# The second expert's values taken from the sum of both experts' activations

## The reference

```
t  = rms_norm(x);  weights = top 2 of softmax(t @ gate), normed
h1[e] = t @ w1 + 2 (t @ a1[e]) @ b1[e];   h3[e] likewise with w3, a3, b3
act[e] = silu(h1[e]) * h3[e]
out = sum over e of weights[e] * (act[e] @ w2 + 2 (act[e] @ a2[e]) @ b2[e])
```

## Time and profile before

| | us |
|---|---|
| median of 3 runs | 1060.06 |
| lowest, highest | 1056.37, 1061.72 |
| profiled execution | 1054.69 |
| its span, first to last instruction | 1053.0 |

### The profile page before, as it was taken

How to read it: one execution, slowest core, us unless ns; L and a number is a source line. 1 busy time by engine, 2 the same in 40 slices (tenths; PEclk the granted TensorE clock), 3 DMA queues, 4 the chain that set the end, 5 groups by cost and what they waited for, 6 DMA issues and landing times. The chain is left out here.

```text
span 1053.0 us, 15574 instructions
## 1 busy us (share of the span) xinstructions
PE 980.6 (93%) x4429; PEld 669.9 (64%) x4429; DVE 711.2 (68%) x2140; ACT 507.9 (48%) x1039; POOL 500.1 (47%) x485
## 2 busy tenths in 40 slices
PE   3999999999999999999999999899988999889993
PEld 2766667656565665656566656477864667648873
DVE  5787779788786877879797776445543667634542
ACT  3433454655646556564453332144534777515451
POOL 3456555554535545354654655524451155423443
PEclk9999999999999999999999999999999999989997
DMA  6069000000000000000000002146534000015651
GB/s 181 1 284 415 3 1 1 1 1 1 1 0 2 0 1 1 1 0 1 12 3 9 11 11 71 39 137 197 166 94 140 1 22 22 22 42 178 194 174 34
DMA packets 42900, 65.12 MB, mean 62 GB/s; under 512 B 7153, under 2 KB 25121, under 8 KB 40640
## 3 DMA queue, kind: packets, MB, share of 16 engines
q1 hardware_dynamic: 37824, 55.59, 16.1%
q0 software_dynamic: 4992, 8.54, 2.4%
HBM read 37.20 MB, written 28.74 MB: 63 GB/s over the span
## 5 line engine op out<-in xcount | busy, mean ns | idle before, releaser
L362 PE MATMUL bank<-split 128*128 128x512 f32 x416 | 206.9, 497 | 7.8 <-DVE ud L1267 4.1
L364 PE MATMUL bank<-split 128*128 128x512 f32 x416 | 165.2, 397 | 0.0
L363 PE MATMUL bank<-split 128*128 128x512 f32 x416 | 164.8, 396 | 0.0
L863 ACT ACTIVATE sil<-bank 128x512 f32<-128x512 f32 x128 | 76.2, 595 | 116.0 <-PE bank L364 115.2
L1644 POOL TENSOR_TENSOR gsum<-act 128x512 f32<-128x512 f32 x64 | 84.9, 1327 | 81.5 <-DVE act L1203 81.4
L421 PE MATMUL bank<-act,a 128*128 128x512 f32 x256 | 117.6, 592 | 0.0
L362 PEld LDWEIGHTS bank<-split 128*128 128x128 f32 x416 | 79.5, 191 | 48.8 <-issue 17.4
L1199 DVE TENSOR_TENSOR act<-bank,sil 128x512 f32<-128x512 f32 x128 | 87.8, 686 | 17.2 <-PE bank L364 14.2
L363 PEld LDWEIGHTS bank<-split 128*128 128x128 f32 x416 | 79.9, 192 | 28.3 <-issue 18.6
L688 PE MATMUL bank<-xlT,e 128*128 128x256 f32 x368 | 91.2, 392 | 5.1 <-ACT xlT L1068 2.7
L1203 DVE TENSOR_TENSOR act<-act,wT 128x512 f32<-128x512 f32 x128 | 91.7, 716 | 4.4
(11 more groups left out here) (283 smaller groups left out, 1957.6 us busy)
## 6 DMA issues: line engine op xcount, KB each, us to landing
e<-e_dram SPq DMA_DIRECT2D x92, 256.0 KB, 3.1
rows_in<-yw SPq DMA_DIRECT2D x17, 1056.0 KB, 17.8
xin<-rows_in SPq DMA_DIRECT2D x46, 132.0 KB, 3.0
x<-rows_out SPq DMA_DIRECT2D x8, 256.0 KB, 4.7
rows_in<-yw,slot_i POOLq DMA_INDIRECT x64, 2.3
rows_out<-ob,ids POOLq DMA_INDIRECT x46, 2.3
out<-ob,ids POOLq DMA_INDIRECT x46, 2.4
act<-b_dram SPq DMA_DIRECT2D x2, 256.0 KB, 3.1
```

Source lines behind the costliest of these rows:

```text
L362: mm(dst, w[0], m[0], start=start, stop=False, **more)
L363: mm(dst, w[0], m[1], start=False, stop=False, **more)
L364: return mm(dst, w[1], m[0], start=False, stop=stop, **more)
L863: af(sil[(k - 1) % 2][:, :], bank[BH1[STEPS[k - 1][0] % 2]][:, :], ACT.Silu).then_inc(silu_done.sem, 1)
```

## The change

The second expert's values are no longer computed from its own activations. `value_sum` multiplies a2 by the sum of both, and the second expert's part comes out as (values of the sum) - (values of the first), so that DVE masks the first expert's values by the difference of the two masks (`mdT`) and POOL subtracts. The sum is made in place of the second expert's activations, then split once: ACT copies the high part (`sums_high`, four a slot), POOL subtracts the low part (`sums_low`, four a slot), and both `value_sum` and `down` use mm3 on it. w2 and a2 are split too, in slot 0 (two copies on ACT, two subtractions on POOL). `down(3)` moves to the next slot, behind `a_den`; on POOL `up_low(0)` moves ahead of `total(3)`. mdT has two buffers and the first mask has one. Seven weights of the second layer are loaded after the last h product, into space that the split weights have left.

```diff
-        mT = [[sb(f"mT{i}{k}", [P, S]) for k in range(2)] for i in range(2)]
-        mdT = sb("mdT", [P, S])
+        mT0 = sb("mT0", [P, S]); mT1 = [sb(f"mT1{i}", [P, S]) for i in range(2)]; mdT = [sb(f"mdT{i}", [P, S]) for i in range(2)]
...
+            gs = [(part(33 + j), part(j)) for j in range(J)]
+            w2s, a2s = parts(37), parts(39)
...
+        act1 = [sb(f"act1{j}", [P, S]) for j in range(J)]
...
+        late_loads = whole(("wk_l1", wk_l1), ("wq_l1", wq_l1), ("wv_l1", wv_l1), ("waT", waT), ("wbT", wbT))
+        late_loads += [(eb1r[:, :], d["eb1"].rearrange("o (n p) -> (o n) p", p=P)), (eb2r[:, :], d["eb2"].rearrange("o (n p) -> (o n) p", p=P))]
...
+                  (w2s, w2[:, :], 1.0), (a2s, a2[:, :, :].rearrange("p j d -> p (j d)"), 1.0)]
+        LOW_DVE, LOW_POOL, LOW_LATE = (0, 1, 3, 5), (2, 4), (6, 7)
@@ sync
                     sp.wait_ge(*h3_ready(MAINS - 1))
+                    for dst, src in late_loads:
+                        sp.dma_start(dst, src).then_inc(late_loaded.sem, 16)
@@ tensor
-                        last = mm(bank[BV][:, :], a2[:, j, :], act_[e][j][:, :], start=j == 0, stop=j == J - 1)
+                        last = mm(bank[BV][:, :], a2[:, j, :], act0[j][:, :], start=j == 0, stop=j == J - 1)
...
+                def value_sum():
+                    if l is None:
+                        return
+                    pe.wait_ge(*r_done(l, 1))
+                    pe.wait_ge(*sum_low(l))
+                    if l == 0:
+                        pe.wait_ge(weight_rest.sem, len(LOW_POOL) + 2)
+                    for j in range(J):
+                        last = mm3(bank[BV][:, :], tuple(w[:, rows(j)] for w in a2s), gs[j], j == 0, j == J - 1)
+                    last.then_inc(v_ready.sem, 1)
+
+                def down(n, j):
+                    if n is None:
+                        return
                     if j == 0:
-                        pe.wait_ge(*xf_done(g - 1))
-                    pe.wait_ge(*summed(g, j + 1))
-                    mm(bank[BOUT][:, :], w2[:, j, :], gsum[j % 2][:, :], start=j == 0, stop=False).then_inc(w2_used.sem, 1)
+                        pe.wait_ge(*xf_done(n - 1))
+                        if n == 0:
+                            pe.wait_ge(weight_rest.sem, len(LOW_POOL) + 1)
+                    pe.wait_ge(*sum_low(n, j + 1))
+                    mm3(bank[BOUT][:, :], tuple(w[:, rows(j)] for w in w2s), gs[j], j == 0, False)
...
                 a_den()
+                down(l, 3)
                 h(3, 2)
                 pre_T()
                 a_back()
-                value(1, range(J))
+                value_sum()
...
                 a_gate(1)
-                down(2)
+                down(g, 2)
                 a_gate(2)
-                down(3)
                 a_gate(3)
@@ scalar
                     if n == 0:
+                        act.wait_ge(*u_masked(q - 1))
+                    if n == 1:
                         act.wait_ge(*r_done(q - 2))
...
+                def sums_high(j):
+                    if g is None:
+                        return
+                    act.wait_ge(*summed(g, j + 1))
+                    act.wait_ge(*v_ready(g - 1))
+                    af(gs[j][0], act1[j][:, :], ACT.Copy).then_inc(sum_high.sem, 1)
...
                 silu(2)
+                sum_weights()
...
                 silu(5)
+                sums_high(0)
...
                 silu(6)
+                sums_high(1)
...
                 silu(8)
+                sums_high(2)
                 up_high(0)
                 a_square(1)
                 a_square(2)
                 a_gates()
                 up_high(1)
+                sums_high(3)
                 a_norm(1)
@@ vector
-                    v.tensor_tensor(r1[:, :], bank[BV][:, :], mT[g % 2][0][:, :], ALU.mult).then_inc(r_done.sem, 1)
+                    v.tensor_tensor(r1[:, :], bank[BV][:, :], mdT[g % 2][:, :], ALU.mult).then_inc(r_done.sem, 1)
@@ gpsimd
                     pool.wait_ge(*weighted(g, STEP[j, 1]))
-                    pool.wait_ge(*w2_used(g, j - 1))
-                    pool.tensor_tensor(out=gsum[j % 2][:, :], in0=act_[0][j][:, :], in1=act_[1][j][:, :], op=ALU.add).then_inc(summed.sem, 1)
+                    pool.tensor_tensor(out=act1[j][:, :], in0=act0[j][:, :], in1=act1[j][:, :], op=ALU.add).then_inc(summed.sem, 1)
+
+                def sums_low(j):
+                    if g is None:
+                        return
+                    pool.wait_ge(*sum_high(g, j + 1))
+                    pool.tensor_tensor(out=gs[j][1], in0=act1[j][:, :], in1=gs[j][0].bitcast(F32), op=ALU.subtract).then_inc(sum_low.sem, 1)
...
-                    pool.tensor_tensor(out=r1[:, :], in0=r1[:, :], in1=r2[:, :], op=ALU.add).then_inc(r_ready.sem, 1)
+                    pool.tensor_tensor(out=r1[:, :], in0=r2[:, :], in1=r1[:, :], op=ALU.subtract).then_inc(r_ready.sem, 1)
...
                 total(1)
+                sum_weights_low()
+                sums_low(0)
                 f_scale()
+                sums_low(1)
                 mask_diff()
                 a_scale()
                 r_scale(s.r_stat)
                 total(2)
+                sums_low(2)
+                up_low(0)
                 total(3)
-                up_low(0)
                 up_low(1)
+                sums_low(3)
                 a_product()
```

More of the change, by code:

```diff
@@ L148, in build @@
         xnT = sb("xnT", [P, S])
+        lower = xnT[:, 0:P]
         lg = sb("lg", [P, T, E]); gt = sb("gt", [P, T, E]); pr = sb("pr", [P, T, E]); mx1 = sb("mx1", [P, 2, T])
@@ L155, in build, with part, parts @@
         rf = sb("rf", [P, T])
+        rows_in = nc.dram_tensor("rows_in", [NROWS, W], F32, kind="Internal").ap()
+        rows_out = nc.dram_tensor("rows_out", [NCH * S, P], F32, kind="Internal").ap()
+        stats_l = sb("stats_l", [P, T, 6]); part_l = sb("part_l", [P, 4, T])
+        mv_l = [sb(f"mv_l{i}", [P, T]) for i in range(2)]; sc_l = [sb(f"sc_l{i}", [P, 2, T]) for i in range(2)]
+        yn_l = [yn_f, yn_a]
+        yT, zT, pr_, pT = [tT, hT], mT1, act0[0:2], act0[2:4]
+        vu = [z, h2]
+        nb_l = sb("nb_l", [P, T]); nmx = sb("nmx", [P, 2]); rs = sb("rs", [P, 2]); rsi = sb("rsi", [P, T])
+        with nc.sbuf_tensor("split", [P, 41 * S], F32R) as split:
+            def part(n):
+                return split[:, n * S:(n + 1) * S]
+            def parts(n):
+                return part(n), part(n + 1)
+            gs = [(part(33 + j), part(j)) for j in range(J)]
+            w1s, w3s, b1s, b3s = (parts(4 + 2 * i) for i in range(4))
+            w2s, a2s = parts(37), parts(39)
+            a1s, a3s = (tuple(split[:, 12 * S + (k + i) * P:12 * S + (k + i + 1) * P] for k in range(2)) for i in (0, 2))
+            ts = [parts(13), parts(15)]
+            uas = [[parts(17 + 8 * p + 2 * i) for i in range(2)] for p in range(2)]
+            uds = [[parts(21 + 8 * p + 2 * i) for i in range(2)] for p in range(2)]
+        act1 = [sb(f"act1{j}", [P, S]) for j in range(J)]
+        act_ = [act0, act1]
+        a1, a3 = act1[0][:, 0:P], act1[0][:, P:2 * P]
+        wk_l1 = sb("wk_l1", [P, P]); wq_l1 = sb("wq_l1", [P, P]); wv_l1 = sb("wv_l1", [P, P])
+        waT = sb("waT", [P, P]); wbT = sb("wbT", [P, P])
+        wak = sb("wak", [P, P]); gmat = sb("gmat", [P, P]); wuT = sb("wuT", [P, P])
         cnt = sb("cnt", [P, E]); cnt_i = sb("cnt_i", [P, E], I32); nt_i = sb("nt_i", [P, E], I32); ntf = sb("ntf", [P, E])
@@ L652, in first_layer @@
                 mask(0)
-                down(0)
+                down(g, 0)
                 a_mid(1)
@@ L658, in first_layer @@
                 a_mid(2)
-                down(1)
+                down(g, 1)
                 mask(2)
@@ L666, in first_layer @@
                 h(3, 8)
-                value(0, (0, 1))
+                value((0, 1))
                 a_gate(0)
@@ L906, in mask, with sum_weights @@
                     ins.then_inc(maskT_saved.sem, 1)
+                def sum_weights():
+                    if g != 0:
+                        return
+                    for n in LOW_LATE:
+                        dst, w, f = SPLITS[n]
+                        af(dst[0], w, ACT.Copy, scale=f).then_inc(weight_high.sem, 1)
+                def sums_high(j):
[4 more added lines that the diff above has]
+                    af(gs[j][0], act1[j][:, :], ACT.Copy).then_inc(sum_high.sem, 1)
                 def up_high(i):
```

83 lines of the change are left out of this document (31 added, 52 removed).

## The result

The changed kernel takes 1103.42 us (median of 4 runs, 1100.97 to 1105.75), the kernel before 1059.44 beside it (4 runs, 1056.37 to 1061.72): a ratio of 1.0417 [1.0381, 1.0453]. The forecast was 1071.8, with a range that ended at 1086. The direction was right; the size was not: +11.7 us forecast, +44.0 measured. The profiled executions took 1054.69 (span 1053.0) and 1105.75 (span 1104.0), so they lie 51 us apart where the medians lie 44: that of before is 5 under its median, that of the changed kernel 2 over.

What follows compares the result with a forecast made beforehand. PE, DVE and ACT were taken as within a microsecond of each other, DVE ending last after the change. Terms 6.0 + 0 + 3.9 + 0 + 1.8 = +11.7 us gave 1066.4 profiled, 1071.8 median; range 1047 to 1086.

Steps and rivals of the forecast that it cites:

- +1.0 in slots 5 to 10, 6.0 us: Gated slots 5 to 10: one new POOL op holding DVE, with ACT's 0.6 mostly beside it, costs +1.0 each, 6.0 us.
- taken as 0: Slots 3 and 4: DVE has spare time; PE's -0.34 against ACT's +0.6, counted as 0.
- POOL's subtractions and DVE: Four more 1.28 us POOL ops per slot, each holding DVE 0 to 1.28; bound +0 to +2.5 per gated slot.
- Rival (c): Port takes it all: both new ops held in each of six slots, +23.7 us, 1083.8; chance 0.13.
- ACT's copies: Four per slot at 0.63; the third, queued before up_high(0), waits for total(2): +0.6 in a gated slot if DVE is on time.
- down(3) moved: Gated slots: moved behind a_den, it leaves a gap nothing fills and costs 0.69 where PE has no gap.
- Slots 0 to 2: First stage without gates: PE waits for POOL's low parts, +0.5 in slot 0, +1.7 each in 1 and 2, +3.9 total.
- Slots 11 to 14: PE's lead about 4.7, -1.4 to +0.3 each; `ud` later by 0 to 1.3: 0 for the four, bounds -5 and +5.
- The way out: End of the layer, after slot 15: POOL's row scatter 2.2 late, some regained from slot 15's products, +1.8.
- At nothing: Late weights, two-buffer mask difference and new addresses count nothing; a few us once without cover, addresses up to 1 us either way.
- Rival (a): PE sets every slot, holds fall into idle time: -11.6 us, 1048.5; chance 0.22.
- (b): Effects cancel: gated slots lose 2.4, way out 1.8, eight other slots win 4 together: 0, 1060; chance 0.2.

Runs made afterwards that it cites:

- experiment 3: Changed kernel without POOL's four subtractions a slot, PE taking the high part in place of the low: 1064.35 us, 1.0042 of the kernel before.
- experiment 2: Kernel before with the new algebra alone (plain products, no splits, copies or subtractions) and down(3) moved into the next slot: 1068.65 us, 1.0087 of before.
- experiment 1: Kernel before with the new algebra alone: plain products, no splits, copies or subtractions, down(3) in its old place: 1059.90 us, 1.0003 of before.
- experiment 9: Changed kernel without subtractions, down(3) back, copies 3 and 4 between sigmoids, POOL's old order, high part again as third pass: 1049.34 us, 0.9900 of before.
- experiment 4: Changed kernel with copies and subtractions elsewhere in the queues and down(2) also in the next slot: 1100.23 us, 1.0386 of the kernel before.
- experiment 5: Changed kernel with POOL's subtractions in place, but PE neither waits for nor reads them: 1101.72 us, 1.0394 of the kernel before.
- experiment 6: Changed kernel with each subtraction replaced by a POOL power on 128x5, low part left out: 1076.57 us, 1.0161 of the kernel before.
- experiment 7: Changed kernel with keep-busy products on PE ahead of the second and fourth gate product: 1103.95 us, 1.0405 of the kernel before.
- experiment 10: Changed kernel's arithmetic with subtractions on DVE, all four down products in the next slot, later copies between sigmoids, POOL's old order: 1099.55 us, 1.0383 of before.
- experiment 11: Changed kernel with subtractions for j = 0 and 1 kept, those for j = 2 and 3 left out: 1089.60 us, 1.0257 of the kernel before.
- experiment 8: Changed kernel with two passes, no subtractions, down(3) back, copies 3 and 4 between sigmoids, POOL's old order: 1038.72 us, 0.9804 of the kernel before.
- experiment 12: Changed kernel with subtractions for j = 2 and 3 kept, those for j = 0 and 1 left out: 1080.63 us, 1.0189 of the kernel before.

## Why the prediction was wrong, step by step

The failed step is the term **"+1.0 in slots 5 to 10, 6.0 us"**, and behind it the sentence "nearest is one op held" for a slot that had four new ones. At full clock slots 5 to 10 lost 14.3 in place of 6.0, 2.4 a slot. Slots 3 and 4, "taken as 0", lost 6.7: there the spare time on DVE that the prediction named did not cover. Of these 21 us, 6.4 come without the subtractions (experiment 3) and about 14.6 with them.

- **POOL's subtractions and DVE.** The mechanism was named, and its size was taken from one held operation in the earlier trace rows. Measured by leaving them out: 39.1 us, 2.4 per slot over 16 slots, in all stages: 22.0 in slots 3 to 10, 7.3 in slots 0 to 2, 7.8 in slots 11 to 14 (sums of the same stretches in the changed kernel and experiment 3). Rival (c), "both new ops held", was nearest in kind and number, with 1083.8; but it too had only the gated slots 5 to 10 lose by it, and looked only at sums_low(0) and (1). The leaky step beside sums_low(2) (684 ns on average before, 1044 after) was not looked for. What I should have added up is the chance of a hold for every wide POOL operation, since DVE works through most of the slot.
- **The rule on the shared ports.** The Trainium skill says ("SBUF — State Buffer", section "SBUF: two separate sides") that of a VectorE instruction with two SBUF inputs and a GpSimd instruction that reads SBUF the later one stands still for the other's whole instruction. The traces agree where POOL reads wide tiles (1.25 for a 128x4 operation that began 0.06 after a mask difference of 1.29), and `ua` with one input from PSUM is not held (683 ns). They differ for tiny tiles: the weighting at 343.64, with both inputs in SBUF, took its usual 0.69 beside the power that ran from 342.49 to 344.50, and 64 powers of 1.40 us added nothing to DVE's busy time (715.6 and 714.4). Here the measurement decides: a long POOL instruction on a tiny tile did not hold DVE for as long as its row says.
- **ACT's copies.** "The third is the dear one, +0.6": the replay had ACT wait 0.97 for total(2) (318.38 to 319.35). It waits 1.52 in slot 7 of experiment 3 and 2.09 in the changed kernel, because total(2) itself came late by DVE's held statistics. The step was right for the queue as it stood and missed that its inputs move.
- **down(3) moved.** "Costs 0.69 where PE has no gap", in the slots with gates only: experiment 2, where it is a plain product, has 0.7 to 0.8 a slot on average in all stages, 8.7 us. The sum had offset it in the gated slots by PE's shorter products; PE's time that becomes free before a wait is not paid out.
- **Slots 0 to 2**: +3.9 forecast (0.5, 1.7, 1.7), +8.1 measured (2.7, 2.8, 2.6), 7.3 of it with the subtractions. The replay from total(2) on was right in kind (waits of 1.59 at h(3,1) and 0.16 at down(3)), but it began at total(2) and so left out the wait before down(1), 1.72 in slot 1.
- **Slots 11 to 14**: 0 forecast, bounds -5 to +5; +5.3 measured. Experiment 3 has 150.2 there, 2.5 under before, so PE's gain did exist; the subtractions took 7.8.
- **The way out**: +1.8 forecast, about +5 beyond the stall that is not the change's (what comes before the first total(0) is in it), some 3 of it with the subtractions. It was not taken apart further.
- **At nothing**: the late weights and the addresses. The new algebra with its mask buffers cost nothing (experiment 1). The late weights were not tried alone; they are in experiment 3 too, where the rest is +2 beyond the stall.
- **Not in the prediction at all**: the granted clock. It was 1.00 in all gated slots before, and the term was missing: about 7.4 us.
- **Rival (a)**, PE sets every slot, and **(b)** fell: PE's 21.8 us are worth 10.1 even without one subtraction (experiment 9).

What was to be seen: PE's wait for the sigmoid grew to 2.76, not 1 (1.35 without the subtractions); waits for the sum's low parts came, in 13 places, 1.4 us on average and at most 3.1; ACT was idle before the third copy; z after the last gate came 0.75 later (12.46 against 11.71), as forecast.

The account of the 44.0 us, by medians of kernels that lie one edit apart: three passes in a good order -10.1; the change's order of down(3), copies and total(3) +15.0; POOL's time for the subtractions +12.2; DVE held beside them +25.2; PE waiting for and reading the low parts +1.7. The clock's 7.4 is inside these, most of it in the 25.2.

## What to carry to other kernels

Before moving elementwise work onto POOL in a kernel where DVE works through most of the loop, price each wide operation at what it holds of DVE (here 0.4 us a piece, 0.3 without the clock's part, against 0.2 for its own time in POOL's queue), not only at POOL's free time: POOL was idle half the time and the work still cost 39 us. The check afterwards is one row: DVE's busy time rising with an unchanged count of instructions. And a saving on the busiest engine is worth its full size only in slots where that engine waits for nobody: here 21.8 us of passes paid 10.1.

## What the runs showed of the hardware

- The hold runs both ways and in turn: four DVE operations stretched from 2.4 to 6.17 us by POOL's up_low, while these went from 1.28 to 1.7.
- The granted clock fell in the gated stretch (to between 0.90 and 0.96 over a slot) in seven kernels, all with subtractions or their stand-ins in the queues (the changed one, experiments 4 to 7, 10 and 11); it was 1.00 in all eight slots of before and of experiments 1, 2, 3, 8, 9 and 12, though 12 has half the subtractions. The slots differ from kernel to kernel, and a slot at 0.96 costs about 1.1 us. In the changed kernel each of the five falls to the 1.2 GHz level begins within a wait of PE or up to 1.2 us after one, waits of 1.7 to 3.1 us. In slot 5 it lasts from 252.1 to 262.4, and a gate product that takes 1.10 in slot 7 takes 2.04:
```profile
252.76 2.04 PE L630 MATMUL bank<-hT,wf_b 128*128 128x512 f32 x2 [2.76 <-ACT gi L1008]
```
Slot 7 has the same wait of 2.76 and slot 9 one of 2.56, without a fall. With the waits at the gates filled (experiment 7), slots 5 to 10 had no fall. What decides which wait goes with a fall stays open.
- At the end of the first layer DVE and ACT stand idle until 723 us with a releaser that the profile calls remote, and PE waits 4.3 for them:
```profile
723.04 0.28 ACT L868 ACTIVATE wak<-bank 128x128 f32<-128x128 f32 x1 [6.42 <-remote]
```
The same wait stands in the profiled executions of all other kernels (3.9 to 4.3) and not in that of before. Its cause was not found; a profiled execution may so be 4 to 5 us from the next with no edit between them.
